# A two-layer block of local attention and feed-forward: W2 taken out of the burst and done one tile per attention step

## What is computed

```python
h = shift_token(x)                       # second 64 channels taken from the token before
q, k, v = split(h @ wqkv)                # 8 heads of 64
q = l2norm(q) * qs ; k = l2norm(k) * ks ; q, k = rotary_xpos(q, k)
x = x + local_attention(q, k, v) @ wo    # windows of 64 keys: own and previous
h = layernorm(shift_token(x)) * lg + lb
a, g = split(h @ w1 + b1)                # 341 each
x = x + (a * gelu(g)) @ w2 + b2
```

## Time and profile before

| what | value |
|---|---|
| median of three runs | 2024.12 us (2023.77 to 2026.48) |
| the profiled execution | 2023.84 us |
| its span, first to last instruction | 2022.0 us |
| TensorE busy | 1660.5 us, 82% |
| VectorE, ScalarE, GpSimd busy | 1419.8, 1157.7, 1091.1 us |
| mean granted TensorE clock | 0.937 of full |
| global attention between the two stacks | some 940 to 1180 us of the span |

### The profile page before, as it was taken

One profiled execution on the slowest core, in us unless ns is written; L12 is line 12 of the kernel. 1 busy time (PEld: TensorE's weight loads), 2 busy tenths in 40 slices (PEclk: granted clock), 3 DMA queues, 4 the chain that ended last, 5 costly groups with the idle time before them and its releaser, 6 DMA issues.

```text
span 2022.0 us, 48409 instructions
## 1 busy us (share of the span) xinstructions
PE 1660.5 (82%) x15864; PEld 1363.3 (67%) x15864; DVE 1419.8 (70%) x3769; ACT 1157.7 (57%) x3315; POOL 1091.1 (54%) x1090
## 2 busy tenths in 40 slices
PE   1898989888989899746756749989897889898984
PEld 1677878776878777525535537777776777777773
DVE  6686868676868687455655648868786768786873
ACT  1676757565757576412312227767675767576671
POOL 2774848464848485221231247757565657566650
PEclk9999999999999999978968979999998999999997
DMA  7231212122212121031010032111122221112113
GB/s 255 66 98 40 47 40 60 47 78 63 47 39 53 39 48 38 12 128 42 0 41 21 0 83 47 44 46 42 49 49 84 50 61 44 49 38 51 36 37 107
DMA packets 183672, 112.13 MB, mean 55 GB/s; under 512 B 86721, under 2 KB 164129, under 8 KB 182945
## 3 DMA queue, kind: packets, MB, share of 16 engines
q1 hardware_dynamic: 183456, 109.12, 20.4%
HBM read 43.41 MB, written 23.42 MB: 33 GB/s over the span
## 4 chain that ended last, share of the span: by engine, by line
PE 68%; DVE 11%; issue 6%; ACT 5%; SPq 3%; DMA 3%; POOL 2%; DVEq 0%; POOLq 0%; ACTq 0%
PE QK L345 12%; PE OB L690 10%; PE TT L578 7%; PE SC L619 6%; PE QK L578 5%; PE OB L645 5%; PE VB L345 4%; DVE o_n L977 4%; PE OB L578 4%; PE TT L345 3%; PE SC L601 2%; ACT probs L1098 2%; PE OB L745 2%; PE VB L745 2%; PE SC L782 2%
## 5 line engine op out<-in xcount | busy, mean ns | idle before, releaser
L1098 ACT ACTIVATE probs<-SC,shift,qgain 128x128 f32<-128x128 f32 x1024 | 457.4, 469 | 96.8 <-DVE shift L896 96.6
L1222 POOL TENSOR_TENSOR ve<-mv,epsilon 128x1 f32<-128x1 f32 x128 | 24.3, 190 | 529.1 <-DVE mv L940 529.1
L345 PE MATMUL QK<-w_qkv,hT 128*128 128x512 f32 x768 | 226.8, 433 | 19.9 <-DMA w_qkv<-qkv_d 10.5
L1098 ACT ACTIVATION_READ_ACCUMULATOR probs<-SC,shift,qgain 128x1 f32 x1024 | 220.0, 215 | 0.0
L1235 POOL TENSOR_TENSOR rnorm<-clip,mhalf 128x8 f32<-128x8 f32 x128 | 211.2, 1650 | 15.0 <-DVE clip L905 14.9
L578 PE MATMUL TT<-ident,probs 128*128 128x128 f32 x1280 | 194.4, 280 | 25.0 <-ACT probs L1098 18.4
L888 DVE TENSOR_REDUCE top<-SC 128x4 f32<-128x512 f32 x256 | 175.4, 685 | 56.0 <-PE SC L619 56.0
L1244 POOL TENSOR_TENSOR qgain<-clip,mhalf 128x8 f32<-128x8 f32 x128 | 209.4, 1636 | 0.0
L578 PEld LDWEIGHTS TT<-ident,probs 128*128 128x128 f32 x1280 | 156.9, 144 | 64.7 <-issue 20.8
L949 DVE TENSOR_TENSOR rope_c<-QK,rope 128x512 f32<-128x512 f32 x256 | 172.9, 676 | 35.9 <-PE QK L345 34.8
L954 DVE TENSOR_TENSOR rope_s<-QK,rope 128x256 f32<-128x256 f32 x512 | 190.3, 412 | 0.0
(11 more groups left out here) (136 smaller groups left out, 3908.6 us busy)
## 6 DMA issues: line engine op xcount, KB each, us to landing
v_prev<-v_own SPq DMA_DIRECT2D x256, 128.0 KB, 2.3
x_att<-stream SPq DMA_DIRECT2D x128, 64.0 KB, 2.1
h<-stream SPq DMA_DIRECT2D x256, 32.0 KB, 1.8
stream<-x_new SPq DMA_DIRECT2D x32, 256.0 KB
w_qkv<-qkv_d SPq DMA_DIRECT2D x3, 1536.0 KB, 6.6
h<-x_mid SPq DMA_DIRECT2D x128, 32.0 KB
h<-x_mid SPq DMA_DIRECT2D x128, 31.8 KB
rope<-rope_d SPq DMA_DIRECT2D x24, 128.0 KB, 3.2
```

Source lines behind the costliest of these rows:

```text
L345: last = mm(dst, fr(left(a)), fr(right(b)), start=(k == 0), stop=(k == 2))
L1098: last = nc.scalar.activation(probs[:, b, hd, :], SC[:, hd * P:hd * P + P], ACT.Exp, bias=shift[:, b, hd:hd + 1], scale=qgain[:, b, hd % 4 ...
```

## The change

W2 becomes a stage of its own at distance 15: step g does W2 of tile g-15, three accumulating matmuls into columns 128 to 255 of OB, beside WO's result in columns 0 to 127 and ahead of it. VectorE adds the residual of one tile (128 columns) behind x_mid. SP stores each half of x_new when its fourth tile is there, so two stores per sequence remain, at other steps, with a semaphore for each half. The burst ends after the W1 pairs. In the step behind a burst TensorE does W2 and WO first, then the first half of the probabilities' transposes and then those of k and q, each behind the act2 product that frees its bank. The values product goes by heads and alternates between the two windows, and so between output halves. GpSimd's x_b2 moves behind k_a. W2's weights get their own semaphore and load. Sixteen steps are now straight code, the loop has six passes, and the drain is seven steps longer.

```diff
@@ -43,7 +43,8 @@
 TH, QKV, TQK, ATT, WO, FFN_IN = 1, 2, 4, 5, 6, 7
 BURST = TILES + FFN_IN - 1
-LAST = (ITERS - 1) * TILES + BURST
+W2 = BURST + 1
+LAST = NT - 1 + W2
 KQV, LN_OUT, LN_IN = 0, 3 * TILES, 4 * TILES
...
@@ -91,17 +92,17 @@
     def burst_of(it, g):
-        if (g - BURST) % TILES or (it is None and g < BURST):
+        if (g - BURST) % TILES or (it is None and not BURST <= g < NT + BURST):
             return None
         n = (g - BURST) // TILES + stack * ITERS
         return n if it is None else it + n
-    for g in range(TILES):
-        step(tile_of(None, g), burst_of(None, g), None)
-    with eng.Fori(1, ITERS) as it:
+    for g in range(2 * TILES):
+        step(tile_of(None, g), burst_of(None, g), burst_of(None, g - 1))
+    with eng.Fori(2, ITERS) as it:
         for j in range(TILES):
             step(tile_of(it, j), burst_of(it, j), burst_of(it, j - 1))
-    for g in range(NT, LAST + 2):
+    for g in range(NT, LAST + 1):
         step(tile_of(None, g), burst_of(None, g), burst_of(None, g - 1))
...
@@ -405,8 +409,10 @@
                     sp.dma_start(w_1[:], w1_d[l]).then_inc(s_ffnw, 16)
                 sp.dma_start(b_1[:], b_1all[:, l]).then_inc(s_ffnw, 16)
                 sp.dma_start(b_2[:], b_2all[:, l]).then_inc(s_ffnw, 16)
+
+            def load_w2(l):
                 for c, (at, n) in enumerate(CH):
-                    sp.dma_start(w_2[0:n, c, :], w2_in[l, at:at + n, :]).then_inc(s_ffnw, 16)
+                    sp.dma_start(w_2[0:n, c, :], w2_in[l, at:at + n, :]).then_inc(s_w2w, 16)
             def load_qkv(l):
                 sp.dma_start(w_qkv[:], qkv_d[l]).then_inc(s_qkvw, 16)
...
@@ -441,36 +447,33 @@
                     before = x_mid[127:128, i - 1, 64:128] if i else zeros[0:1, 0:64]
                     sp.dma_start(h2[0:1, k, 64:128], before).then_inc(s_h2[k], 16)
-            def store(l, s, n):
-
-                for half in range(2):
-                    need(sp, s_xn, n * 2 + (half + 1))
-                    a, b = half * HALF, (half + 1) * HALF
-                    sp.dma_start(rows(stream[l + 1, s, 1 + a * P:1 + b * P, :]), x_new[:, a:b, :]).then_inc(s_st, 16)
+            def store(l, s, half, n):
+
+                need(sp, s_xn, n * TILES + HALF * (half + 1))
+                a, b = half * HALF, (half + 1) * HALF
+                sp.dma_start(rows(stream[l + 1, s, 1 + a * P:1 + b * P, :]), x_new[:, a:b, :]).then_inc(s_st[half], 16)
             def stack(k):
                 first = k * ITERS
-                def iteration(it, c, l, s, lb, sb_, at=(), after_burst=None):
+                def iteration(it, c, l, s, lb, sb_, at=()):
                     for j in range(TILES):
                         def tile(skew):
                             n = j - skew + c
                             return Tile(it, n, k) if it is not None or 0 <= n < NT else None
                         if l is not None:
-                            if not isinstance(l, int) or l > 0:
-
-                                if j == 0:
-                                    need(sp, s_st, (first - 1 + (c // TILES if it is None else it)) * 32 + 16)
+                            if j == 0 and (not isinstance(l, int) or l > 0):
+
+                                for half in range(2):
+                                    need(sp, s_st[half], (first + (c // TILES if it is None else it) - SEQS + 1) * 16)
                             loads(tile(0), l, s)
                         for when, do in at:
                             if when == j:
                                 do()
                         moves(tile)
-                        if j == BURST - TILES and lb is not None:
-                            store(lb, sb_, (c // TILES if it is None else it) - 1 + first)
-                            if after_burst:
-                                after_burst()
+                        if lb is not None and j % HALF == (W2 + HALF - 1) % HALF:
+                            store(lb, sb_, j // HALF, (c // TILES if it is None else it) - 2 + first)
                 def wait_tile(s_, n, unit=1):
                     need(sp, s_, (n + k * NT + 1) * unit)
...
@@ -519,14 +523,27 @@
                     wait_tile(s_y, m + TILES - 1)
                     load_wo(1)
-                iteration(None, m + TILES, 1, 0, 0, SEQS - 1,
-                          [(0, rope_after(5)), (1, rope_after(6)), (2, after_qkv), (2, rope_after(7)), (6, after_wo)],
-                          lambda: load_ffn(1))
-                with sp.Fori(SEQS + 1, ITERS) as it:
-                    iteration(it, 0, 1, it - SEQS, 1, it - SEQS - 1)
-                for g in range(NT, LAST + 1):
+                def after_ffn_in():
+                    need(sp, s_act2, (first + SEQS) * 6)
+                    wait_tile(s_xb2, m + TILES - 1)
+                    load_ffn(1)
+
...
...
@@ -620,30 +638,60 @@
                                       start=False, stop=True, skip_group_check=True)
                 last.then_inc(s_s, 1)
+            def qk_transposed(tile, t):
+                b = t.i % 2
+                pe.wait_ge(s_qr, t.count())
+                pe.wait_ge(s_kr, t.count())
+                if t2 := tile(QKV + 1):
+                    pe.wait_ge(s_rot, t2.count())
+                    pe.wait_ge(s_sq, t2.count())
+                for m, src in ((1, k_r), (0, q_r)):
+                    for c in range(PAIRS):
+                        last = transpose(QK[:, m * 512 + c * P:m * 512 + c * P + P], src[:, b, c * P:c * P + P])
+                    last.then_inc(s_tqk, 1)
+
+            def w2_tile(tile, t):
+                i = t.i
+                if i == 0:
+                    pe.wait_ge(s_w2w, t.loads() * 48)
+                if i % HALF == 0:
+                    need(pe, s_act2, t.count(every=TILES, unit=6) - 3 * (1 - i // HALF))
+                if t2 := tile(WO):
+                    pe.wait_ge(s_oT, t2.count())
+                else:
+                    pe.wait_ge(s_xn, t.count(back=1))
+                for c, (at, m) in enumerate(CH):
+                    last = mm(OB[:, P:2 * P], act2[0:m, i // HALF, c, i % HALF * P:i % HALF * P + P],
+                              w_2[0:m, c, :], start=(c == 0), stop=(c == 2))
+                last.then_inc(s_w2, 1)
+
+            def projected(t):
+                if t.i == 0:
+                    pe.wait_ge(s_wow, t.loads() * 16)
+                pe.wait_ge(s_oT, t.count())
+                for c in range(PAIRS):
+                    last = mm(OB[:, 0:DIM], oT[:, c, :], w_o[:, c, :], start=(c == 0), stop=(c == PAIRS - 1))
+                last.then_inc(s_y, 1)
+
             def step(stack):
                 def f(tile, burst, before):
-                    if t := tile(TQK):
-                        b = t.i % 2
-                        pe.wait_ge(s_qr, t.count())
-                        pe.wait_ge(s_kr, t.count())
-                        if t2 := tile(QKV + 1):
-                            pe.wait_ge(s_rot, t2.count())
-                            pe.wait_ge(s_sq, t2.count())
-                        for m, src in ((1, k_r), (0, q_r)):
-                            for c in range(PAIRS):
-                                last = transpose(QK[:, m * 512 + c * P:m * 512 + c * P + P], src[:, b, c * P:c * P + P])
-                            last.then_inc(s_tqk, 1)
-                    if t := tile(ATT):
-                        probs_transposed(t, 0)
+                    if before is None:
+                        if t := tile(TQK):
+                            qk_transposed(tile, t)
+                        if t := tile(ATT):
+                            probs_transposed(t, 0)
+                    if t := tile(W2):
+                        w2_tile(tile, t)
                     if t := tile(WO):
-                        if t.i == 0:
-                            pe.wait_ge(s_wow, t.loads() * 16)
-                        pe.wait_ge(s_oT, t.count())
-                        if before is not None:
-                            pe.wait_ge(s_xn, before * 2 + 2)
-                        for c in range(PAIRS):
-                            last = mm(OB[:, 0:DIM], oT[:, c, :], w_o[:, c, :], start=(c == 0), stop=(c == PAIRS - 1))
-                        last.then_inc(s_y, 1)
+                        projected(t)
+                    if before is not None:
+
+                        pe.wait_ge(s_act2, before * 6 + 5)
+                        if t := tile(ATT):
+                            probs_transposed(t, 0)
+                        pe.wait_ge(s_act2, before * 6 + 6)
+                        if t := tile(TQK):
+                            qk_transposed(tile, t)
                     if t := tile(QKV):
                         i, b = t.i, t.i % 2
                         if i == 0:
...
@@ -663,8 +711,6 @@
                         if t2 := tile(FFN_IN + 1):
                             pe.wait_ge(s_h2l, t2.count())
-                        if before is not None:
-                            pe.wait_ge(s_xn, before * 2 + 1)
```

(60 more changed lines are left out.)

33 lines of the change are left out of this document (25 added, 8 removed).

## The result

| kernel | median | runs | range |
|---|---|---|---|
| before | 2025.01 us | 5 | 2023.77 to 2031.08 |
| changed | 2009.51 us | 5 | 2007.74 to 2012.29 |

The ratio is 0.9919, 95% interval 0.9901 to 0.9936. The forecast was 1974 us with a range from 1944 to 2006. The direction was right, the size was not, and the time lies outside the range.

What follows compares the result with a forecast made beforehand. Three closed loops decide a step: TensorE's own (9.54 us), GpSimd with VectorE, ScalarE with TensorE. The terms -49 - 11 + 1 + 7.6 - 6 + 8 give -49.4 us, so 1974 us, range 1944 to 2006.

Steps and rivals of the forecast that it cites:

- joins: Step behind the burst: k_r's transposes 3.38 us earlier, values product 0.75, later Gelu +0.63; -3.5 each, -49 us in all.
- loop ends: Returns of the loop: one fewer per stack, -11 us; W2 and values product at the ten remaining, +1 us.
- plain steps: Steps without burst or loop return: 9.68 us against a mean of 9.59, +0.09 in each of 84, +7.6 us.
- steps ahead of the first W2: Eight per stack that have only the gains: about 9.15 us against 9.54, -6 us over 16.
- drain: End of each stack: eight one-tile W2 steps of 1.28 us, 10.2 us; +4 us per stack, +8.
- GpSimd loop: GpSimd and VectorE, shift's end to q_r's end, 9.66 us: loses 0.41, gains about 0.2, becomes about 9.45.
- ScalarE loop: ScalarE and TensorE through exponentials, hT, oT and WO: 9.02 us plus W2's 0.65, about 9.68; decides the plain step.
- Rival 2: Plain steps take 9.95 us as x_b behind k_a meets VectorE's clips and loops delay each other: 1997 us, 18%.
- later Gelu: Burst's own step: Gelu table load 2.7 us behind o_n against 2.07, so the W1 chain starts 0.63 later.
- rival 3: Values product's halves do not run in pairs; TensorE's loop is 10.19 us: 2031 us, slower, 8%.
- rival 4: Longer straight code brings its own issue waits or remaining returns grow, losing the 11 us: 1985 us, 9%.
- Rival 1: Plain steps stay at 9.45 us because the ScalarE loop is looser than summed: 1946 us, 20%.

Runs made afterwards that it cites:

- its second: Changed kernel with the W2 tile behind h2n's transpose, where TensorE waits for o_n, x_new behind the second shift, h2n and x_b2 also moved: 1953.8 us.
- the drain mended: Kernel with W2 beside o_n, plus the eight W2 tiles behind a stack's last burst alternating between two banks: 1937.5 us, ratio 0.9583.

## Why the prediction was wrong in size

The spans differ by 11.5 us (2022.0 to 2010.5) where the sum said 49.4. The distances between o_n's starts give each term (with their fractions they come to -11.2):

| term of the sum | predicted | measured | how |
|---|---|---|---|
| joins | -49 | -35 | 14 x (22.52 - 25.03) |
| loop ends | -10 | -9 | the steps with a return (12) or the change of layer (2), sum 220.0, before; 10, 2 and two plain ones, 210.6, after |
| plain steps | +8 | +24 | 68 x (9.99 - 9.64) |
| steps ahead of the first W2 | -6 | -4 | 9.72 and 9.34 against 9.93 and 9.59, 9 steps each |
| drain | +8 | +14 | last o_n to the next stack's first 8.6 longer, to the end 6.3, start-up 1.2 shorter |

**The step that failed** is the plain step: "The GpSimd loop loses x_b (0.41, the distance from 261.57 to 261.98) because x_b now stands behind k_a, where GpSimd has the 1.61 us hole" and "So the ScalarE loop decides: 9.68". Each loop was summed as if its instructions kept their lengths, while the same edits moved two of them onto each other: from o_n's start h2n moved from 7.25 us (255.86 to 263.11) to 8.11 (246.82 to 254.93), as W2's tile and x_new stand ahead of the rotary, but k_r only from 7.85 to 8.18, as x_b2's 0.41 had left its path. Between them had been 0.26 us. The runs put 0.24 us a step on that meeting. Without it the step is 9.75, and the loop that decides is the one named, 0.07 above the forecast. The prediction had such a meeting before it: it read shift at 0.76 us where q_r ended, "though it normally takes far less", and did not ask which others the edit would make. Rival 2 had the right size, 9.95 for 9.99, and the right suspect in x_b2's move, but named VectorE's clips and not h2n, so the size is luck; it got 18%, and alone it would have given 1997. The prediction also counted 84 plain steps where 68 are of that kind, and its upper bound is low by its own terms: 1997 and 14 x 0.8 for the join make 2008, not 2006.

**The join.** Its first part came out: the transposes of k_r 1.99 us behind the last W1 product (268.36 to 270.35) with 1.97 predicted, the second half of the transposed probabilities 6.95 behind it, with 6.93 predicted (188.93 less 178.62, less 3.38). Waits on act2 cost nothing. The later Gelu was right in kind: the table load comes 2.88 behind o_n (256.93 to 259.81), with 2.7 predicted and 2.07 before. What failed is "Behind that the values product gives 0.75 more": o_n stood behind a shift that met k_a. From the table load to the next o_n were 22.95 us before and are 19.65 in the changed kernel, 3.3 less, and they are 19.65 too with the old values order: there the product's 0.75 is worth nothing, and as its Gelu isn't late the join is even shorter (21.86). With x_b2 back this stretch is 18.84, 4.1 less as the sum had it, and the join 21.57, its -3.5.

**The drain.** From the first of the last W2 products to the last x_new were 6.25 us before (856.37 to 862.62). In the second stack they are 10.9 now (1980.31 to 1991.23), +4.7 with +4 predicted, so "1.28 x 8" was right at full clock. In the first they are 14.1 (844.44 to 858.58), +7.9: five tiles at the lower clock took 0.73 us more each, for which the sum had no term.

**Right.** The halves do run in pairs. Timeline of the changed kernel:

```profile
255.60 0.22 PE L738 MATMUL OB<-v_prev,pT 128*64 128x64 f32 x1
255.61 0.22 PE L738 MATMUL OB<-v_own,pT 128*64 128x64 f32 x1
255.66 0.22 PE L738 MATMUL OB<-v_prev,pT 128*64 128x64 f32 x1
```

From the first, at 255.49, to h's transpose at 256.58 are 1.09 us, with 1.08 predicted. The rule of the Trainium skill ("TensorE: Matmul & The Clock Gate", Part 3, The mechanism) that the prediction weighed against it (a weight load overlaps matmuls in flight only at another row group) doesn't hold here. Each alternation of output halves overlaps, though all loads use all rows, and rival 3 fell with it; its own number, 2031 us without the pairs, was measured as 2029. The waits of TensorE answer to the earlier trace rows (us in total, times, longest):

```profile
PE QK L596 <- issue: 36.9, 10, 3.9
...
PE OB L664 <- ACT oT L1121: 12.6, 64, 0.7
```

Ten returns as predicted, and elsewhere only the waits on issue that were there before (VB, 2.9 us in both kernels), so rival 4 fell too. W2 waits for oT (0.2 us each, 64 times) as predicted. Rival 1, plain steps of 9.45, fell as well: the ScalarE loop is longer than summed, not shorter.

## What to carry to other kernels

Summing each engine's loop is not enough when an edit shifts engines against each other: list which VectorE and GpSimd instructions on SBUF stand within half a microsecond of each other before, and ask where the edit puts them. Two pairs met here, h2n with k_r and shift with k_a. Work that is to fill a gap belongs where the profile shows the engine waiting (TensorE behind o_n), not ahead of the product for which the next stage waits. Split a change into its parts before judging it: here two lines of it were worth 38 us, the unrolling 12, and W2's move lost time in its first place and won 19 in its second (1972.8 to 1953.8), some 31 to 35 with the drain mended (by the ratios and by the medians).

## What I had not expected of the hardware

- A 128x128 VectorE operation from SBUF takes 0.72 to 1.20 us instead of 0.34 when it meets a 1.04 us GpSimd operation, and a four-column one 1.18 instead of 0.16. Such a length in a row is a wait that no view of waits lists.
- In the drain the changed kernel's granted clock fell to 0.50 in one stack, and a tile of six matmuls went from 1.3 to 2.04 us; in the other stack, with the same waits, it stayed at 1.00. Without the waits it stayed at 1.00 in both.
